# Keys turned by 32x32 blocks and a pass through DRAM in 14 of 24 items, with two rectified chunks an item on GpSimd

## What is computed

```python
def _layernorm(x, w, b): ...
for i in range(6):                                   # 6 layers
    xn = _layernorm(x, ln1_w[i], ln1_b[i])
    q, k, v = xn @ wq[i], xn @ wk[i], xn @ wv[i]     # 8 heads of 16 features
    q = softmax(q, axis=-1)                          # over the 16 features of a head
    k = softmax(k, axis=-2)                          # over the 1024 tokens
    context = einsum('bhnd,bhne->bhde', k, v)
    x = einsum('bhnd,bhde->bhne', q, context) @ wo[i] + bo[i] + x
    xn = _layernorm(x, ln2_w[i], ln2_b[i])
    hdn = xn @ w1[i]                                 # 128 -> 512
    x = where(hdn >= 0, hdn, 0.01 * hdn) @ w2[i] + x
# beside it, once: a top-1 mixture of 8 experts (128x128 each) on the normalised input
out = x_in + x * silu(expert_output)
```

## Time and profile before

| | us |
|---|---|
| median of 3 runs | 596.42 (594.59 to 596.98) |
| time of the profiled execution | 596.75 |
| its span, first to last instruction | 594.9 |
| TensorE busy with matmuls | 578.7 |
| VectorE busy | 540.1 |
| ScalarE busy | 434.8 |
| GpSimd busy | 311.1 |

### The profile page before, as it was taken

The page is one execution under the profiler, slowest core; times in us unless marked ns, Lnnn a source line. Parts: engine busy times, 40 slices in busy tenths (PEclk is TensorE's granted clock), DMA queues, the critical chain, the costliest instruction groups (busy, mean ns, idle before and its releaser), DMA issues.

```text
span 594.9 us, 12614 instructions
## 1 busy us (share of the span) xinstructions
PE 578.7 (97%) x4166; PEld 516.3 (87%) x4166; DVE 540.1 (91%) x1352; ACT 434.8 (73%) x763; POOL 311.1 (52%) x308
## 2 busy tenths in 40 slices
PE   7999999999999999999999999999999999999897
PEld 7899897887978889889889898898898898898796
DVE  6887999999988999999999999999999999988865
ACT  2658595876976868868768768768779678687652
POOL 5896134755852772442442532433523766867752
PEclk9989999999999999999999999999999999999999
DMA  8209233323224154445435435445342351441102
GB/s 282 75 10 328 72 110 121 124 94 130 95 84 152 71 152 146 112 133 169 124 123 163 109 141 150 116 163 158 103 165 80 108 167 57 129 156 62 45 36 106
DMA packets 74946, 73.20 MB, mean 123 GB/s; under 512 B 27265, under 2 KB 65153, under 8 KB 74882
## 3 DMA queue, kind: packets, MB, share of 16 engines
q1 hardware_dynamic: 72400, 68.18, 35.6%
q0 software_dynamic: 2048, 4.20, 2.3%
q10 hardware_dynamic: 434, 0.02, 0.0%
HBM read 39.87 MB, written 32.51 MB: 122 GB/s over the span
## 4 chain that ended last, share of the span: by engine, by line
PE 75%; DVE 11%; DMA 4%; issue 3%; POOL 3%; ACT 2%; SPq 1%; DVEq 0%; ACTq 0%; POOLq 0%
PE psY L513 23%; PE psH L406 6%; PE psS L558 6%; PE psH L407 6%; PE psH L408 6%; PE psT L592 6%; PE psT L401 6%; PE psT L526 5%; PE psM L538 5%; DVE st L1295 2%; PE psS L455 2%; DMA through<-blocks 1%; DVE X L1563 1%; DVE hid L1553 1%; DMA turned<-through 1%
## 5 line engine op out<-in xcount | busy, mean ns | idle before, releaser
L513 PE MATMUL psY<-w_all,hid 128*128 128x128 f32 x1536 | 188.7, 276 | 2.5 <-DVE hid L1553 1.8
L513 PEld LDWEIGHTS psY<-w_all,hid 128*128 128x128 f32 x1536 | 182.0, 193 | 6.6 <-issue 2.3
L1553 DVE TENSOR_TENSOR hid<-psH,hsl 128x512 f32<-128x512 f32 x192 | 127.2, 676 | 13.6 <-ACT hsl L936 13.1
L936 ACT ACTIVATE hsl<-psH 128x512 f32<-128x512 f32 x192 | 108.3, 591 | 42.0 <-PE psH L408 38.5
L2038 POOL TENSOR_TENSOR rstd<-veps,minus_half 128x8 f32<-128x8 f32 x44 | 72.7, 1653 | 61.2 <-DVE veps L1312 61.0
L2134 POOL TENSOR_TENSOR qsm<-qe,qrec 128x1024 f32<-128x1024 f32 x24 | 46.5, 1938 | 97.8 <-DVE qrec L1636 97.8
L2112 POOL TENSOR_TENSOR xn_lo<-xn,xn_hi 128x512 fp32r<-128x512 f32 x48 | 60.6, 1282 | 69.4 <-ACT xn_hi L1000 69.4
L406 PE MATMUL psH<-xn_hi,w_hi 128*128 128x512 f32 x192 | 86.4, 450 | 3.7 <-DVE hid L1553 3.4
L966 ACT ACTIVATE xh<-X,shift,rstd 128x128 f32<-128x128 f32 x188 | 77.0, 482 | 8.9 <-POOL shift L2041 8.7
L408 PE MATMUL psH<-xn_lo,w_hi 128*128 128x512 f32 x192 | 76.1, 396 | 0.0
L407 PE MATMUL psH<-xn_hi,w_lo 128*128 128x512 f32 x192 | 76.0, 396 | 0.0
(11 more groups left out here) (161 smaller groups left out, 1024.9 us busy)
## 6 DMA issues: line engine op xcount, KB each, us to landing
through<-turn SPq DMA_DIRECT2D x22, 512.0 KB, 2.7
turn<-through SPq DMA_DIRECT2D x88, 128.0 KB
through<-blocks SPq DMA_DIRECT2D x20, 512.0 KB, 3.2
turned<-through SPq DMA_DIRECT2D x80, 128.0 KB, 2.8
wb<-expert_rows SPq DMA_DIRECT2D x40, 128.0 KB, 2.0
sorted_x<-blocks SPq DMA_DIRECT2D x5, 512.0 KB, 4.4
xs_xsT<-sorted_x SPq DMA_DIRECT2D x40, 64.0 KB, 2.5
sorted_y<-ys SPq DMA_DIRECT2D x10, 256.0 KB, 2.4
```

The lines of the kernel that those rows point to most:

```text
L513: last = nc.tensor.matmul(tile(psY, t), tile(hid[:, c, :], t), w2_all[:, n // NBATCH, c, :], start=(c == 0 and t == 0), stop=(c == NC - 1) ...
L936: nc.scalar.activation(hsl[:, i % 2, :], psH[:, i % 2, :], ACT.Copy, scale=SLOPE) \
L1553: nc.vector.tensor_tensor(hid[:, i % NC, :], psH[:, i % 2, :], hsl[:, i % 2, :], ALU.max) \
```

## The change

Three things are done, and with them every engine's order is written anew.

**Keys.** For items 9 to 22 (`attention_turned`) TensorE's 8 transposes and ScalarE's copy of them are dropped. In their place VectorE turns exp(keys) by 32x32 blocks (`blocks_of_keys`) into the first quarter of `xraw` (which holds the input of sequence 0, so that is loaded again at the end, `load_input_again`), and SyncE passes it through DRAM into `expkT` in the way that was used for xh1 and xh2. `key_sums` reads it with a strided pattern.

**Chunks 2 and 5 of items 7 to 20** (`pooled`): ScalarE writes 0.01 h to `hsl` and relu(0.99 h) to `hid`, and GpSimd adds the two; VectorE has nothing to do with them. max(h, 0.01 h) = 0.01 h + relu(0.99 h).

**SyncE** issues the store of xh1's blocks ahead of the loads of xh2's, and loads of weights at the start stand in another order.

```diff
+        TURNED_FIRST, TURNED_END = 9,23
+        POOLED = (2, 5,)
+        POOLED_FIRST, POOLED_END = 7, 21
...
+            def store_blocksk(n):
+                if attention_turned(n):
+                    k = turned_before_a(n)
+                    sp.wait_ge(sig("blocksk_ready"), k + 1)
+                    wait(sp, "turnedk_ready", 16 * NQ * k)
+                    sp.dma_start(throughk, blocksk).then_inc(sig("throughk_ready"), 16)
+            def load_turnedk(n):
+                if attention_turned(n):
+                    k = turned_before_a(n)
+                    sp.wait_ge(sig("throughk_ready"), 16 * (k + 1))
+                    wait(sp, "g_done", n)
+                    quadrants(expkT, throughk, "turnedk_ready")
...
             def slot(s):
                 groups(s)
-                feature_major2(s - 2)
-                feature_major1(s)
+                store_blocksk(s - 1)
+                load_turnedk(s - 1)
+                store_blocks2(s - 2)
+                store_blocks1(s)
+                load_turned2(s - 2)
+                load_turned1(s)
...
@@ hidden (TensorE), and the same in slope (ScalarE)
-                    wait(pe, "hid_ready", NF * n + i - 1)
+                    if pooled(*two_before(n, i)):
+                        pe.wait_ge(sig("h_copied"), pooled_before(*two_before(n, i)) + 1)
+                    else:
+                        wait(pe, "hid_ready", by_vector_before(*two_before(n, i)) + 1)
@@ key_sums (TensorE)
-                    pe.wait_ge(sig("expkT_ready"), n + 1)
+                    if attention_turned(n):
+                        pe.wait_ge(sig("turnedk_ready"), 16 * NQ * (turned_before_a(n) + 1))
...
-                        last = nc.tensor.matmul(psS[:, 0:D], tile(xh1[:, n % 2, :], t), tile(expkT, t),
+                        e = by_tile(expkT[:, :])[:, t] if attention_turned(n) else tile(expkT, t)
+                        last = nc.tensor.matmul(psS[:, 0:D], tile(xh1[:, n % 2, :], t), e,
@@ slope (ScalarE)
+                        if pooled(n, i):
+                            act.wait_ge(sig("y_done"), NF * n + i - 3)
+                            nc.scalar.activation(hid[:, i % NC, :], psH[:, i % 2, :], ACT.Relu, scale=1.0 - SLOPE) \
+                                .then_inc(sig("h_copied"), 1)
@@ VectorE
+            def blocks_of_keys(n):
+                if attention_turned(n):
...
+                    dve.wait_ge(sig("expk_ready"), n + 1)
...
+                    nc.vector.transpose(blocksk, by_block(expk[:, :])).then_inc(sig("blocksk_ready"), 1)
...
+                add_attention(s - 1)
+                statistics2(s - 1)
+                add_y(s - 3, 1)
+                statistics1(s + 1, 1)
+                key_maxima(s)
+                variances1(s + 1)
+                blocks_of_keys(s)
@@ GpSimd
+            def leaky(n, i):
+                if pooled(n, i):
+                    pool.wait_ge(sig("h_copied"), pooled_before(n, i) + 1)
+                    nc.gpsimd.tensor_tensor(hid[:, i % NC, :], hid[:, i % NC, :], hsl[:, i % 2, :], ALU.add) \
+                        .then_inc(sig("hid_pooled"), 1)
```

892 lines of the change are left out of this document (502 added, 390 removed).

## The result

The changed kernel takes **656.9 us** (median of 4 runs, 655.84 to 660.96) against 596.38 for the kernel before in the same comparison: ratio 1.103, 95% interval 1.098 to 1.109. The forecast was 620, range 607 to 634. The direction was right; the loss is 2.6 times what was forecast. The profiled execution took 656.18 us, its span is 654.5.

A forecast was written before the change was run, and what follows sets the result against it. TensorE bounds the kernel at 22.9 us a slot; the new chain attention, VectorE, DRAM, key sums closes at 24.8. Ten slots of 24.8 and four of 24.0 make 344.0 against 320.6: 596.75 + 23.4 = 620, range 607 to 634.

The forecast's parts named there:

- What bounds the kernel: Before the change TensorE sets the time without spare, 22.94 us for a slot with an expert group; VectorE is close behind.
- the rival of no change: TensorE has idle time hidden behind overlapping records, so dropping the transposes gives nothing: 597 us, chance 0.05.
- TensorE's work: Per slot, 0.87 us of transposes go and 0.24 for hidden chunks standing alone comes: 22.94 falls to 22.3 us.
- The strided reading of the keys: TensorE's key sums read the turned keys with a stride; taken at nothing, 0.2 us a slot if it cost a tenth.
- The relus: ScalarE gains two relus an item, 0.59 us each if they cost what a slope does; its room holds them.
- GpSimd's adds: GpSimd gains two adds, nearest row 1282 ns, lying beside other work as long as chunk 2 is ready in time.
- The chain up to add_y: On VectorE, from add_attention through the statistics of norm 2 to add_y: 4.23 us, read from the earlier trace.
- (a): VectorE's leaky of chunk 0 waits behind the keys' turn; TensorE stalls 1.8 us at chunk 2, attention ends at 24.1 to 24.2.
- (b): Keys pass through DRAM in 7.25 to 8.7 us, about 7.9; key sums wait, attention ends at 24.1 to 25.5, middle 24.7.
- Nothing lost in prologue and end: Before and behind the repeating slots the work is the same in another order: 0 us, 4 either way.
- The longer chain: Slower DRAM passes, keys delayed by xh1's pass and GpSimd's late chunk make slots 26 to 26.5 us: 640, chance 0.1.

The follow-up runs named there:

- before_low8: The kernel before, with GpSimd's low parts of items 2 and later cut to 8 of 512 columns a half: 591.5 us, ratio 0.992.
- order_only: The changed kernel with keys transposed by TensorE and chunks 2 and 5 on VectorE again, leaving only the new engine orders: 655.6 us, ratio 1.096.
- load2_early: The changed kernel with SyncE's loads of xh2's blocks back ahead of the store of xh1's: 651.4 us, ratio 1.089.
- the last exchange: The changed kernel with VectorE's last half of norm 2 moved ahead of a gate product at the end: 659.0 us, ratio 1.098.
- low8: The changed kernel with GpSimd's low parts of items 2 to 23 cut to 8 of 512 columns a half: 630.2 us, ratio 1.052.
- no_pooled: The changed kernel with chunks 2 and 5 of items 7 to 20 on VectorE again, keys still through DRAM: 657.0 us, ratio 1.099.

## Why the prediction was wrong

**What bounds the kernel.** Right: before_low8 shortens VectorE's path by 0.5 us a slot and leaves the slot at 22.9. TensorE had nothing to spare, and the rival of no change falls. The rule of the Trainium skill that the prediction cites from "Perfetto Trace Analysis" on the busy share of weight loads (40.45 of 45 us) pointed the wrong way here.

**TensorE's work.** Half a microsecond too low. In the slot shown, by distances from start to start, there are gaps of 1.1 us ahead of the keys (327.27, with four outputs of 3.57 from 322.60) and 2.25 ahead of the third hidden chunk (334.53, with queries of 1.78 from 330.50). 26.18 less these is 22.8, where 22.3 was forecast. From the key sums to attention it takes 5.67 in most slots with an expert part, where 7.1 - 1.8 = 5.3 was forecast. The strided reading of the keys cost nothing, as taken: 1.82 us to the next start, against 1.79 in order_only without it. The relus (0.59) and GpSimd's adds (1.28) took what was forecast, too.

**The chain up to add_y.** This is the step that failed. The prediction took "4.23" from the earlier trace rows as a fixed cost and GpSimd's low parts at nothing. 4.23 is no property of the instructions: they take 3.82 with GpSimd out of the way, 4.23 where its low parts touch them a little, and 5.25 in the mean (up to 6.10) where they lie wholly on them. The change moved them there: ScalarE's normalising of xh2, which they wait for, now waits for its loads 16 times and 32.9 us in all (3 times and 5.4 us before), since the loads stand behind a store; load2_early brings these waits to 12.2 us and y down to 4.39. The term was mis-sized by 1.0 us a slot, 14 us, and the 4.23 already held 0.4 of it.

The signal stood in the profile of before, where the first of these instructions (L1302) took 0.41 us in the mean and its neighbours of the same form 0.16 and 0.20; I had not asked why. The Trainium skill, "SBUF — State Buffer", section "Who interferes with whom", has the rule: VectorE and GpSimd share a port pair, and a VectorE instruction with two SBUF inputs contends for it with a GpSimd one that reads SBUF; the one that issues second stands still until the first is done. The traces agree for L1432 (1.25 us beside a low part of 1.28) and L1652 (5.45), both with two inputs in SBUF. The same section names tensor_scalar among the instructions that can take both ports and then contend; the last exchange, in which L1487 is one, agrees. That order decides isn't seen there: the records of L1652 and L1487 start 0.13 and 0.64 us ahead of GpSimd's product, and they are the ones that stood still. By that rule the low parts would have been a rival; two of 1.28 us make its price up to 2.5 us a slot.

**(a), leaky 0 behind the turn.** Right in place: TensorE waits there in all 14 slots, 31.5 us in the changed kernel and 17.2 in low8, 1.2 a slot where 1.8 was forecast. In the mean of the 14 slots way (a) came to 334.2 / 14 = 23.87, and 26.20 was measured. Of the 2.3 between, 1.0 is y, 0.15 the rest of the way to the third hidden chunk, 0.7 the stretch from there to the key sums and 0.4 the one behind them. The 0.7 is a second term that the prediction put at nothing. It had no price for what follows a wait: TensorE's clock fell after it in 7 slots of 14, and filling the wait gives 0.6 of the 0.7 back.

**(b), the pass through DRAM.** Wrong in size and in place. It took 7.1 to 7.2 us in the mean where 7.9 had been taken over from xh1. With 7.2 the forecast's own sum has the keys there at 16.9, and TensorE at 17.0. In the changed kernel no key sum of the 14 slots waited for it. The 0.7 us a slot that (b) put on top of (a) was not there.

**Nothing lost in prologue and end.** Wrong by 13.4 us. Of the 8.3 behind item 22, load2_early gives back 3.8 by SyncE's order. The end is 2.1 shorter in low8, which may be the same part. The 5.1 ahead of item 8 are there in every kernel with the new prologue (215.6 to 218.8) and in none with the old (210.0 to 211.5). Which piece of the prologue makes them wasn't tried.

**The longer chain** (640) named slots of 26 to 26.5, which is what came, but mostly for other reasons. Of its three, xh1's pass did delay the keys (5.3 us in 7 slots); GpSimd's chunk made TensorE wait in two slots, 1.2 us; and the keys' passes were not slower than those of xh1. Low parts and clock are not among them. With prologue and end it would have been 653.

**What stays open.** The low parts explain the slots' loss only in the order of the changed kernel. Why order_only, without the turn of the keys (1.2 us on the chain) and with y at 4.60, is as slow is only partly settled: its measured chain, above, has leaky 2 behind the queries' maximum and a turn, and in the changed kernel that chunk is GpSimd's. no_pooled, which puts it back on VectorE and keeps the turn, is no slower, with 0.9 less in y. Which pieces of the order close these loops was not found; undoing the ones that were tried left 25.1 of 26.3 us. No kernel that does all the work beat the one before.
